# Decoder megakernel: earlier and smaller exchanges in cross-attention, four weight places in self-attention, and the bookkeeping of a top-k search moved to another engine

## The chip, the cores and the metric

The kernel runs on one core of one Trainium2 chip as a single launch. The metric is device time in microseconds. The engines are named as the profile names them: PE (matmuls; PEld is its weight load), DVE, ACT, POOL (GpSimd) and SP, which here only issues DMAs. ACT and POOL issue DMAs too. Each engine runs its own instructions strictly in order and waits on semaphores.

## The reference

Two decoder layers on x (4 batches of 512 tokens, 512 wide) with a layer norm behind each of six blocks. The change touches three of them:

```python
x = _layernorm(x + _L0_attn_ref(x, ...))                  # self-attention, 16 heads of 32   (touched)
x = _layernorm(x + _L0_xattn_ref(x, ctx_512, ctx_512))    # cross-attention                  (touched)
x = _layernorm(x + _L0_ffn_ref(x, ...))                   # ternary weights, 8-bit activations
x = _layernorm(x + _L1_attn_ref(x, ...))                  # self-attention                   (touched)
x = _layernorm(x + _L1_xattn_ref(ctx_512, x, ...))        # learned graph                    (touched)
x = _layernorm(x + _L1_ffn_ref(x, ...))                   # 16 experts, top 2

# cross-attention: queries are x itself, keys and values the context, no weights
H, KV = (32, 8); D = 16; G = H // KV
scores = einsum('bkgsd,bktd->bkgst', qh, kh) / sqrt(D); weights = softmax(scores, axis=-1)
out = einsum('bkgst,bktd->bkgsd', weights, vh)

# graph: keep the 153 largest of each row's 512, mix with x through gamma
topk_vals = lax.top_k(sim, 153)[0]; mask = sim >= topk_vals[:, :, -1:]
A = sigmoid(sim) * mask; A = (A + A.T) * 0.5
return (1 - gamma) * x + gamma * A
```

## The kernel before

The program is a row of stages, one behind another, each its own Python function with its own tiles and semaphores: self-attention (tiles `L_attn_...` in the profile, for both layers), cross-attention (`x_...`), FFN (`ffn_...`), self-attention again, graph (`graph_...`), experts. x itself stays in SBUF as the tile `X` (also called `XF`), 16 tiles of 128 tokens by 512.

**Self-attention** loads four 512x512 weight matrices one after another through two staging places `WS`, both inside the tile `PT` (L154). ACT rounds each to `WH` (L293), DVE subtracts to get the rest `WL` (L366), and SP may load the third and the fourth only when `WL` of the first and the second has been made. Order of the matrices: value, query, key, output. A list `plan`, written out by the host code, is the order in which PE, ACT and DVE go through their work.

**Cross-attention** works on 32 groups, g = 0 to 31: group g is batch g // 8 and key head j = g % 8, with four query heads. Operands are split in a high and a low part, since a product is made of three passes. Both parts of the transposed x of a batch (`XTH`, `XTL`, 1 MB each) are *exchanged*: SP writes them to DRAM (L707, L709), waits until they have landed (semaphore `x_out`), and reads them back, stacked by head, into `KS`-shaped rows: `stack_keys` (L726) for the context and `stack_queries` (L719) for x, the latter one group at a time, three groups ahead, into a ring `QS` of four places. In a group PE makes eight `max` units (L979: scores into `M`), DVE reduces each to the row's maximum (L919, `negm`), PE transposes the maxima (`mt`), DVE casts them to `mT` (L928), and SP sends `mT` as one more row of `QS` (`shift_row`, L732). Then PE makes the 16 score tiles `T` (L999), ACT takes their exponentials `PT` (L868), PE multiplies by V into `O` (L1008), ACT copies `O` to `OS` (L881), PE turns it (`turn`) and DVE divides into `Z`. L881 runs once for each group, so its rows are a clock of the groups.

The same `plan` puts the two units `xt` (PE's transposes of the next batch's x, L969, and DVE's and ACT's split of them) in group 4 of a batch. SP's exchange of it stands at the head of group 5. Ahead of group 0, SP loads the whole context (`CT`, `CTOK`, 1 MB each), exchanges its two parts and x of batch 0, and stacks keys, then queries.

Behind the last group of a batch, POOL adds x to `Z` (L828), and DVE makes the moments of the layer norm in small steps laid between its `max` reductions: four `bn_stats` (L94), then some twenty small operations (L64 to L77), two steps per `max` unit from the sixth unit on (`delay`, `pending`). POOL then applies the norm (L831). Between these, POOL sums the FFN weights and cuts twelve pieces of them to ternary (`cut_weights`, L815 to L822). ACT adds up absolute values of the same weights in 24 pieces (L874), four in each of groups 0 to 5.

**Graph**: a search by halving finds each row's threshold, for 16 tiles of rows at once, in 16 halvings (`HALVINGS`). In one halving DVE makes the middle of the interval (L1614), counts the elements above it in tiles 0 to 7 (L1617), ACT counts in tiles 8 to 15 (L1579), and DVE moves the ends (L1621, L1624, L1627, L1628):

```python
with dve.Fori(0, HALVINGS) as n:
    ve.tensor_tensor(mid[:], low[:], width[:], ALU.add).then_inc(q["mid_done"], 1)
    ...
    inst.then_inc(q["counted_v"], 1)
    dve.wait_ge(q["counted_v"], n + 1)
    ...
    dve.wait_ge(q["counted_a"], n + 1)
```

Behind it ACT takes sigmoids (L1595) and scales x (`XS`, L1599), DVE masks (L1650), PE transposes and DVE sums, mixes (L1665) and normalises.

## Time and profile before

| | us |
|---|---|
| median of 3 runs | 2621.11 (2618.74 to 2622.66) |
| the profiled execution, its own time | 2620.35 |
| its span | 2618.3 |
| L0 self-attention | 0 to 484.2 |
| cross-attention | 484.2 to 1044 |
| FFN | 1044 to 1439 |
| L1 self-attention | 1439 to 1920 |
| graph | 1920 to 2110 |
| experts | 2110 to 2618 |

The page gives PE 77% busy, PEld 52%, DVE 67%, ACT 48% and POOL 27% of the span. These are averages over stages with different limits: in cross-attention PE is busy 399.6 of 559.8 us and DVE 379.3, in the graph stage DVE 152.9 of 190, ACT 122.3 and POOL nearly nothing. A row of a timeline reads: start, duration (both us), engine, line, operation, what is written <- what is read, number of instructions, and in brackets the idle time ahead of it with what ended it.

### The profile page before, as it was taken

How to read it: one execution, taken by the hardware profiler on the slowest of the kernel's cores; microseconds unless marked ns; L12 is line 12 of the kernel's file. 1: busy time of each engine (PE TensorE's matmuls, PEld its weight loads, DVE VectorE, ACT ScalarE, POOL GpSimd, SP SyncE). 2: the span in 40 equal slices, each digit the busy share in tenths (PEclk: the TensorE clock that was granted, in tenths of full speed). 3: DMA queues.
4: the chain of work that ended last, by engine and by line, in shares of the span. 5: the costliest groups of instructions: out<-in, count | busy, mean ns of one | idle time of the engine just before them, and what ended most of it. 6: DMA issues, size and time to landing. Idle time of an engine off the chain costs nothing. (4 is left out here: it accounts for less than half of the span.)

```text
span 2618.3 us, 32959 instructions
## 1 busy us (share of the span) xinstructions
PE 2004.7 (77%) x12124; PEld 1350.8 (52%) x12156; DVE 1760.9 (67%) x2783; ACT 1258.8 (48%) x2244; POOL 718.3 (27%) x662
## 2 busy tenths in 40 slices
PE   5999999377778785888894699999910279879990
PEld 4778777222222221455552578777610157657770
DVE  3446565376768685799997445556568865379986
ACT  2323232177556564477777232323348541169881
POOL 1111222203595930211111120232200004055535
PEclk8899999688889888999996699999965589889995
DMA  5332321555352420400000432323110030099976
GB/s 153 83 72 53 70 60 39 159 149 152 85 157 73 147 51 10 175 1 1 1 1 1 121 71 52 73 50 74 25 64 0 0 116 1 1 387 422 415 285 192
DMA packets 84584, 264.55 MB, mean 101 GB/s; under 512 B 17504, under 2 KB 19040, under 8 KB 73424
## 3 DMA queue, kind: packets, MB, share of 16 engines
q0 software_dynamic: 29632, 151.50, 17.3%
q1 hardware_dynamic: 53776, 110.75, 14.9%
q8 instruction: 97, 1.59, 0.2%
q14 instruction: 55, 0.45, 0.1%
q10 hardware_dynamic: 1024, 0.26, 0.0%
HBM read 169.87 MB, written 41.72 MB: 81 GB/s over the span
## 5 line engine op out<-in xcount | busy, mean ns | idle before, releaser
L919 DVE TENSOR_REDUCE x_negm<-x_M 128x2 f32<-128x1024 f32 x256 | 309.3, 1223 | 111.3 <-PE x_M L979 110.8
L868 ACT ACTIVATE x_PT<-x_T 128x512 f32<-128x512 f32 x512 | 280.0, 598 | 197.3 <-PE x_T L999 192.0
L326 ACT ACTIVATE L_attn_PT<-L_attn_T 128x512 f32<-128x512 f32 x320 | 175.7, 595 | 359.5 <-PE L_attn_T L557 359.4
L407 DVE TENSOR_REDUCE L_attn_negm<-L_attn_M 128x2 f32<-128x1024 f32 (+1 forms) x192 | 192.2, 1040 | 58.6 <-PE L_attn_M L538 58.5
L233 POOL DMA_DIRECT2D L_attn_QKS<-L_attn_HL x64 | 34.9, 545 | 596.9 <-ACT L_attn_HL L311 563.1
L999 PE MATMUL x_T<-x_QS,x_KS 49*128 49x512 f32 x512 | 140.0, 544 | 64.7 <-ACT x_PT L868 44.9
L555 PE MATMUL L_attn_T<-L_attn_QKS 97*128 97x256 f32 (+3 forms) x512 | 166.8, 387 | 8.3 <-DMA L_attn_QKS<-L_attn_mT 6.2
L999 PEld LDWEIGHTS x_T<-x_QS,x_KS 49*128 49x128 f32 x512 | 51.8, 199 | 213.3 <-ACT x_PT L868 131.6
L536 PE MATMUL L_attn_M<-L_attn_QKS 96*128 96x384 f32 (+2 forms) x384 | 139.6, 434 | 28.8 <-DVE L_attn_XTL L381 11.5
L1008 PE MATMUL x_O<-x_PT,x_V 128*32 128x512 f32 x1024 | 153.4, 673 | 8.6 <-issue 8.4
L979 PE MATMUL x_M<-x_KS,x_QS 48*128 48x512 f32 x512 | 118.3, 459 | 42.6 <-DMA x_QS<-x_xl 22.8
L1567 PE MATMUL graph_P<-ident,graph_L 128*128 128x128 f32 x64 | 15.7, 427 | 172.6 <-DVE graph_L L1650 164.0
L2187 DVE TENSOR_TENSOR slots_WL<-slots_RAW,slots_WH 128x1024 fp32r<-128x1024 f32 x94 | 114.2, 1216 | 13.6 <-ACT slots_WH L2147 13.6
L557 PE MATMUL L_attn_T<-mask_kq,identr 128*128 128x128 f32 x512 | 121.8, 250 | 0.0
L2125 POOL DMA_INDIRECT slots_XG<-moe_x_rows,moe_slot_token x47 | 75.5, 1607 | 143.1 <-DVE slots_WL L2206 82.5
L555 PEld LDWEIGHTS L_attn_T<-L_attn_QKS 97*128 97x128 f32 x512 | 106.1, 207 | 15.3 <-DMA L_attn_QKS<-L_attn_mT 7.5
L435 DVE RECIPROCAL L_attn_AQ<-L_attn_DEN 128x512 f32<-128x512 f32 (+1 forms) x34 | 107.4, 3160 | 8.2 <-PE L_attn_O L581 8.2
L464 PE MATMUL L_attn_M<-L_attn_XTH,L_attn_WH 128*128 128x512 f32 x256 | 107.2, 419 | 6.1 <-DVE L_attn_WL L366 6.1
L557 PEld LDWEIGHTS L_attn_T<-mask_kq,identr 128*128 128x128 f32 x512 | 107.3, 210 | 0.2
L1579 ACT ACTIVATE graph_seen_a<-graph_SIM,graph_mid 128x512 bf16<-128x512 f32 x128 | 90.5, 708 | 32.5 <-DVE graph_mid L1614 18.9
L2147 ACT ACTIVATE slots_WH<-slots_RAW 128x1024 fp32r<-128x1024 f32 x94 | 94.2, 1058 | 22.6 <-DMA slots_RAW<-in_experts,moe_weight_row 22.6
L536 PEld LDWEIGHTS L_attn_M<-L_attn_QKS 96*128 96x128 f32 x384 | 81.3, 212 | 45.8 <-DVE L_attn_XTL L381 14.5
(389 smaller groups left out, 5528.3 us busy)
## 6 DMA issues: line engine op xcount, KB each, us to landing
L_attn_QKS<-L_attn_HL SPq DMA_DIRECT2D x192, 128.0 KB, 4.7
L_attn_QKS<-L_attn_HL POOLq DMA_DIRECT2D x192, 128.0 KB, 4.1
moe_y_rows<-slots_YS SPq DMA_DIRECT2D x47, 256.0 KB
x_WRAW<-in_w_gateT POOLq DMA_DIRECT2D x8, 1024.0 KB, 7.2
x_QS<-x_xh SPq DMA_DIRECT2D x128, 64.0 KB, 2.4
x_WRAW<-in_w_upT POOLq DMA_DIRECT2D x8, 1024.0 KB, 5.2
x_WRAW<-in_w_downT POOLq DMA_DIRECT2D x8, 1024.0 KB, 6.2
ffn_w<-x_WTER POOLq DMA_DIRECT2D x12, 512.0 KB, 3.5
```

The lines of the kernel that those rows point to most:

```text
L326: ac.activation(PT[:, s, bank], T[:, bank], ACT.Exp, scale=SCALE).then_inc(t_free, 1)
L407: last = ve.tensor_reduce(negm[:, g % 2, h0:h0 + nh, i], src, AX.X, ALU.max, negate=True)
L435: ve.reciprocal(AQ[:, cols], DEN[:, cols]).then_inc(inverted, 1)
L536: pe.matmul(m[:, c:c + w], QKS[0:R, r, 0, h, P * i:P * (i + 1)], QKS[0:R, r, 1, h, 0:w], start=True, stop=False)
L555: pe.matmul(T[:, c:c + w], QKS[0:R + 1, r, 1, h, P * j:P * (j + 1)], QKS[0:R + 1, r, 0, h, P * j:S], start=True, stop=False)
L557: last = pe.matmul(T[:, c:c + P], C["identr"][:], C["mask_kq"][:], start=False, stop=True)
L868: ac.activation(PT[:, s // 4, head(s), :], T[(STEPS_S * g + s) % 3][:], ACT.Exp, scale=SCALE).then_inc(t_free, 1)
L919: ve.tensor_reduce(negm[:, g % 2, u // 4:4:2, u % 4], m[:].rearrange("p (r k) -> p r k", r=2), AX.X, ALU.max, negate=True).then_inc(m_free, 1)
L979: last = pe.matmul(m[:, BANK * r:BANK * (r + 1)], QS[rows, g % 4, u // 4, P * (u % 4):P * (u % 4 + 1)], KS[rows, g % KV, :], start=True, s ...
L999: pe.matmul(T[(STEPS_S * g + s) % 3][:], KS[rows, g % KV, P * j:P * (j + 1)], QS[rows, g % 4, head(s) % 2, :], start=True, stop=True).then ...
L1008: last = pe.matmul(O[VW * h:VW * (h + 1), :], V[:, (g // KV) % 2, j, g % KV, :], PT[:, j, h, :], start=(j == 0), stop=(j == NT - 1))
L2187: ve.tensor_tensor(WL[t % 2][:, cols], RAW[t % RING][:, cols], WH[t % 2][:, cols].bitcast(F32), ALU.subtract).then_inc(up_lo, 1)
```

## The change

**Self-attention.** Four staging places instead of two: the second is the tile `V`, the fourth again the first. The key weights no longer wait for a `WL`; the output weights wait for the first; DVE writes `V` only when two `WL` are made.

**Cross-attention, head.** The context of batch 0 alone (256 KB) is loaded first; x of batch 0 is exchanged in halves, and only the first half is waited for; the context's keys of batch 0 are exchanged and stacked from ACT's queue; the rest of the context, of `CTOK` and of x follows behind the queries of group 2, and the exchange of the context's rest at g = 1, with DVE's split of it behind the first `turn` and ACT's at step 12 of group 0. PE waits for POOL's memsets only ahead of the first `max`. The 24 pieces of absolute sums move to groups 1 to 6.

**Cross-attention, exchange.** The `xt` units move to group 3 of a batch, the exchange into group 4 behind the queries of group g + 3, with no wait behind it; the wait for `x_out` and the keys come in group 5.

**Cross-attention, norm.** POOL's sum of x comes ahead of the ternary pieces, of which 2, 3 and 3 then stand ahead of the norm's application and 2, 1 and 1 behind it. The moments are one step per `max` unit and start at the fifteenth.

**Graph.** The loop is written out; each halving is two interleaved halves of 4 tiles for DVE and 4 for ACT; POOL does all the bookkeeping of the ends, and once a halving scales one tile of x in place, in place of ACT's 16 `XS`. Gamma is loaded and its sigmoid taken first.

```diff
-        if in_batch == 4 and s in (11, 13) and b + 1 < NB:
+        if in_batch == 3 and s in (11, 13) and b + 1 < NB:
...
-                sp.wait_ge(x_out, 32 * (b + 1))
...
+            unload_first_x(0)
+            sp.wait_ge(x_out, 32)
             stack_queries(0)
             stack_queries(1)
...
                 if j == 5 and b + 1 < NB:
-                    unload_x(b + 1)
-                    stack_keys(b + 1, 0, 4)
+                    sp.wait_ge(x_out, 32 * (b + 3))
+                    if b == 0:
+                        sp.wait_ge(ctx_out, 64)
+                    stack_keys(sp, b + 1, 0, 4)
                 if g + 3 < GROUPS:
                     stack_queries(g + 3)
+                if j == 4 and b + 1 < NB:
+                    unload_x(b + 1)
...
-            for b in range(NB - 1):
-                cut_weights((range(0, 2), range(2, 7), range(7, 12))[b])
+            for b, (ahead, behind) in enumerate(((range(0, 2), range(2, 4)), (range(4, 7), range(7, 8)),
+                                                 (range(8, 11), range(11, 12)))):
                 pool.wait_ge(m_free, drained("turn", KV * b + KV - 1))
                 gp.tensor_tensor(Z[b % 2][:], Z[b % 2][:], X[:, b, :, :], ALU.add).then_inc(added, 1)
+                cut_weights(ahead)
...
                     delay -= 1
                     if delay < 0:
-                        next(pending, None)
                         next(pending, None)
...
-                        delay, pending = 5, layernorm_moments(b)
+                        delay, pending = 14, layernorm_moments(b)
...
+        @block.gpsimd
+        def _(pool):
+            PER = 6
+            for g in range(2):
+                gp.tensor_tensor(side(mid, g), side(low, g), side(width, g), ALU.add).then_inc(q["mid_made"], 1)
+            for n in range(HALVINGS):
+                for g in range(2):
+                    step = Steps(pool, q["halving"], 2 * n + g, PER)
+                    pool.wait_ge(q["counted_v"], 2 * n + g + 1)
+                    step(gp.tensor_scalar(side(take, g)[:, 0], side(count, g)[:, 0], TOPK - 0.5, None, ALU.is_ge))
+                    pool.wait_ge(q["counted_a"], 2 * n + g + 1)
+                    step(gp.tensor_scalar(side(take, g)[:, 1], side(count, g)[:, 1], S + 1.5 - 2 * TOPK, None, ALU.is_le))
+                    step(gp.tensor_tensor(side(take, g), side(take, g), side(width, g), ALU.mult))
+                    step(gp.tensor_tensor(side(low, g), side(low, g), side(take, g), ALU.add))
+                    step(gp.tensor_scalar(side(width, g), side(width, g), 0.5, None, ALU.mult))
+                    step(gp.tensor_tensor(side(mid, g), side(low, g), side(width, g), ALU.add))
+                    pool.sem_inc(q["mid_made"], 1)
+                if n == 0:
+                    pool.wait_ge(q["gam2"], 2)
+                gp.tensor_scalar(XF[:, n, :], XF[:, n, :], g2[:, 0:1], 1.0, ALU.mult, ALU.mult).then_inc(q["scaled"], 1)
...
+            for n in range(HALVINGS):
+                for h in range(2):
+                    act.wait_ge(q["mid_made"], 2 * n + h + 1)
+                    for t in range(DVE_TILES + HALF * h, DVE_TILES + HALF * (h + 1)):
```

The order in which SP issues at the head of cross-attention; names are tiles and DRAM buffers, `x0_` is the prefix of the stage. Before:

```order
L701 DMA x0_CT<-in_ctxT 128x4x512
L702 DMA x0_CTOK<-in_ctx_512 128x16x128
L736 DMA x0_ch<-x0_CH 128x2048
L738 DMA x0_cl<-x0_CL 128x2048
L707 DMA x0_xh0<-x0_XTH 128x2048
L709 DMA x0_xl0<-x0_XTL 128x2048
L726 DMA x0_KS<-x0_ch 16x4x512
L726 DMA x0_KS<-x0_cl 16x4x512
```

After, the same queue:

```order
L712 DMA x0_CT<-in_ctxT 128x512
L723 DMA x0_xh0<-x0_XTH 128x1024
L725 DMA x0_xl0<-x0_XTL 128x1024
L734 DMA x0_QS<-x0_xh0 16x2x512 x2
L734 DMA x0_QS<-x0_xl0 16x2x512
```

The first queries stand behind 1.25 MB of other transfers instead of 6 MB and six DMAs of keys; the rest comes behind the queries of group 2.

SP's queue at the first exchange of a next batch. Before:

```order
L732 DMA x0_QS<-x0_mT 1x8x128 x2
L707 DMA x0_xh1<-x0_XTH 128x2048
L709 DMA x0_xl1<-x0_XTL 128x2048
L726 DMA x0_KS<-x0_ch 16x4x512
L726 DMA x0_KS<-x0_cl 16x4x512
L726 DMA x0_KS<-x0_ch 16x4x512 x2
```

After:

```order
L734 DMA x0_QS<-x0_xl0 16x2x512
L716 DMA x0_xh1<-x0_XTH 128x2048
L718 DMA x0_xl1<-x0_XTL 128x2048
L740 DMA x0_QS<-x0_mT 1x8x128 x2
L705 DMA x0_KS<-x0_ch 16x4x512
L705 DMA x0_KS<-x0_cl 16x4x512
```

A row of maxima (`mT`) now stands between the writing of x and the keys, and the wait for the written x stands behind that row.

POOL around the first norm of cross-attention. Before:

```order
L805 TENSOR_SCALAR x0_cut<-ffn_wmean 128x3 x2
L815 TENSOR_SCALAR x0_WTER<-x0_WRAW0,x0_cut 128x2048
L816 TENSOR_SCALAR x0_WTER<-x0_WRAW0,x0_cut 128x2048
L776 DMA x0_WRAW0<-in_w_gateT 128x2048
L820 TENSOR_TENSOR x0_WTER<-x0_WTER 128x2048
```

After:

```order
L822 TENSOR_SCALAR x0_cut<-ffn_wmean 128x3 x2
L845 TENSOR_TENSOR x0_Z0<-x0_Z0,X 128x2048
L832 TENSOR_SCALAR x0_WTER<-x0_WRAW0,x0_cut 128x2048
L833 TENSOR_SCALAR x0_WTER<-x0_WRAW0,x0_cut 128x2048
```

The sum of x (L845, L828 before) went from behind the first two ternary pieces to ahead of them.

## Rows read from the trace of the kernel before

**Rows 1.** Timeline of the head of L0 self-attention, ACT and DVE.

```profile
22.95 1.92 ACT L293 ACTIVATE L_attn_WH<-L_attn_PT 128x2048 fp32r<-128x2048 f32 x1 [5.51 <-DMA L_attn_PT<-in_L_attn_WkT]
...
25.39 0.69 DVE L389 TENSOR_TENSOR L_attn_V<-L_attn_M,L_attn_BR 128x512 f32<-128x512 f32 x1 [2.19 <-PE L_attn_M L464]
...
26.00 2.28 DVE L366 TENSOR_TENSOR L_attn_WL<-L_attn_PT,L_attn_WH 128x2048 fp32r<-128x2048 f32 x1
```

**Rows 2.** Timeline of the head of cross-attention, PE and SP.

```profile
493.50 3.68 PE L969 MATMUL x_M<-ident,X 128*128 128x128 f32 x16 [21.28 <-POOL x_V L770]
...
499.60 0.32 SPq L709 DMA_DIRECT2D x_xl<-x_XTL  x1
...
509.43 0.32 SPq L726 DMA_DIRECT2D x_KS<-x_ch  x1
...
519.97 1.22 PE L979 MATMUL x_M<-x_KS,x_QS 48*128 48x512 f32 x4 [22.79 <-DMA x_QS<-x_xl]
...
534.03 0.79 PE L999 MATMUL x_T<-x_QS,x_KS 49*128 49x512 f32 x2
```

**Rows 3.** Timeline of ACT's L881, once for each group: the clock of the groups.

```profile
613.60 0.62 ACT L881 ACTIVATE x_OS<-x_O 128x512 f32<-128x512 f32 x1
...
636.77 0.60 ACT L881 ACTIVATE x_OS<-x_O 128x512 f32<-128x512 f32 x1
...
677.45 0.61 ACT L881 ACTIVATE x_OS<-x_O 128x512 f32<-128x512 f32 x1
...
701.71 0.60 ACT L881 ACTIVATE x_OS<-x_O 128x512 f32<-128x512 f32 x1
...
745.95 0.60 ACT L881 ACTIVATE x_OS<-x_O 128x512 f32<-128x512 f32 x1
...
782.30 0.61 ACT L881 ACTIVATE x_OS<-x_O 128x512 f32<-128x512 f32 x1
...
809.02 0.60 ACT L881 ACTIVATE x_OS<-x_O 128x512 f32<-128x512 f32 x1
...
828.02 0.60 ACT L881 ACTIVATE x_OS<-x_O 128x512 f32<-128x512 f32 x1
```

**Rows 4.** Window of one undisturbed group: length, busy us of PE, PEld, DVE, ACT, POOL; clock.

```profile
714.82:727.94 13.12, 10.73 (x71) 3.63 (x69) 10.65 (x15) 9.07 (x19) 13.12 (x5) 1.00 0.11 31
```

**Rows 5.** Timeline of the first exchange, SP and PE.

```profile
615.10 0.32 SPq L726 DMA_DIRECT2D x_KS<-x_ch  x1
...
621.91 1.33 SPq L732 DMA_DIRECT2D x_QS<-x_mT  x2
...
630.48 0.79 PE L999 MATMUL x_T<-x_QS,x_KS 49*128 49x512 f32 x2 [5.53 <-DMA x_QS<-x_mT]
```

**Rows 6.** Timeline of DVE at the first norm of cross-attention.

```profile
681.11 1.42 DVE L94 BATCH_NORM_STATS2 x_x_ln_stats<-x_Z 128x6 f32<-128x512 f32 x2 [4.82 <-POOL x_Z L828]
```

**Rows 7.** Timeline of DVE in the search, one halving apart.

```profile
1947.27 0.17 DVE L1614 TENSOR_TENSOR graph_mid<-graph_low,graph_width 128x16 f32<-128x16 f32 x1 [0.37 <-DVE graph_width L1628]
...
1954.28 0.17 DVE L1614 TENSOR_TENSOR graph_mid<-graph_low,graph_width 128x16 f32<-128x16 f32 x1 [0.36 <-DVE graph_width L1628]
```

**Rows 8.** Groups by line and shape: line, engine, op, shapes xcount | busy us, mean ns | idle.

```profile
L1579 ACT ACTIVATE graph_seen_a<-graph_SIM,graph_mid 128x512 bf16<-128x512 f32 x128 | 90.5, 708 | 32.5 <-DVE graph_mid L1614 18.9 <-DMA graph_SIM<-graph_sim 13.6
...
L1617 DVE TENSOR_SCALAR_CACHE_REDUCE graph_seen_v<-graph_SIM,graph_mid 128x512 bf16<-128x512 f32 x128 | 86.6, 742 | 0.6
...
L1137 POOL TENSOR_SCALAR ffn_take<-ffn_count 128x8 f32<-128x8 f32 x18 | 4.3, 238 | 89.4 <-ACT ffn_CT L1177 88.5
...
L1146 POOL TENSOR_SCALAR ffn_XQF<-X,ffn_xscale 128x512 f32<-128x512 f32 x16 | 11.9, 741 | 15.6 <-DVE ffn_uscale L1261 12.8 <-POOL ffn_mid L1141 2.1 <-POOL ffn_mid L1130 0.4
...
L269 POOL TENSOR_SCALAR X<-X,L_attn_L_attn_ln_mean,L_attn_L_attn_ln_rstd 128x512 f32<-128x512 f32 x24 | 49.5, 2070 | 51.0 <-DVE L_attn_L_attn_ln_rstd L77 51.0
...
L1368 DVE TENSOR_SCALAR X<-X,ffn_mean,ffn_rstd 128x512 f32<-128x512 f32 x16 | 8.8, 548 | 0.6
```

**Rows 9.** Timeline of POOL's small operations beside DVE's L1368.

```profile
1430.33 0.53 POOL L1140 TENSOR_SCALAR graph_width<-graph_width 128x8 f32<-128x8 f32 x1
```

More of the change, by code:

```diff
@@ L159, in stage_self_attention @@
         DEN = ps("DEN", [P, BANK])
-        w_in = [sem("w_in0"), sem("w_in1")]
+        w_in = [sem(f"w_in{w}") for w in range(4)]
         w_hi, w_lo, b_in = sem("w_hi"), sem("w_lo"), sem("b_in")
@@ L247, in _ @@
             sp.dma_start(WS[1], wts[ORDER[1]]).then_inc(w_in[1], 16)
[L248 to L250 removed]
+            sp.dma_start(WS[2], wts[ORDER[2]]).then_inc(w_in[2], 16)
+            sp.wait_ge(w_lo, 1)
+            sp.dma_start(WS[3], wts[ORDER[3]]).then_inc(w_in[3], 16)
             sp.wait_ge(ones_set, 2)
@@ L695, in stage_cross_attention, with stack_keys @@
         drained = lambda kind, arg: at[kind, arg] + 3
+        def stack_keys(queue, b, lo, hi):
+            for r in range(2):
+                for n, part in enumerate((0, 1, 0)):
+                    rows = slice(LOW * r + HD * n, LOW * r + HD * (n + 1))
+                    src = CP[part][HD * lo:HD * hi, b, :].rearrange("(j d) s -> d j s", d=HD)
+                    queue.dma_start(KS[rows, lo:hi].bitcast(F32), src).then_inc(keys[lo], 16)
         block = ctx.enter_context(nc.Block())
@@ L719, in stack_queries @@
                         sp.dma_start(QS[rows, g % 4].bitcast(F32), src).then_inc(stacked[g % 4], 16)
-            def stack_keys(b, lo, hi):
-                for r in range(2):
-                    for n, part in enumerate((0, 1, 0)):
-                        rows = slice(LOW * r + HD * n, LOW * r + HD * (n + 1))
-                        src = CP[part][HD * lo:HD * hi, b, :].rearrange("(j d) s -> d j s", d=HD)
-                        sp.dma_start(KS[rows, lo:hi].bitcast(F32), src).then_inc(keys[lo], 16)
             def shift_row(g):
@@ L868, in _ @@
                     ac.activation(PT[:, s // 4, head(s), :], T[(STEPS_S * g + s) % 3][:], ACT.Exp, scale=SCALE).then_inc(t_free, 1)
-                    if g < 6 and s % 4 == 2:
-                        piece = 4 * g + s // 4
+                    if 1 <= g < 7 and s % 4 == 2:
+                        piece = 4 * (g - 1) + s // 4
                         c, half = piece // 2, piece % 2
@@ L956, in _ @@
         def _(t):
-            t.wait_ge(ones_set, 4)
             for x in plan:
@@ L1544, in stage_graph @@
         PP = [ps(f"P{i}", 2 * BANK) for i in range(4)]
-        names = ("loaded mid_done counted_v counted_a gam gam2 "
-                 "sigm xs masked turned summed halved z_done stat norm shifted applied between")
+        names = ("loaded mid_made counted_v counted_a halving scaled gam gam2 "
+                 "sigm masked turned summed z_done stat norm shifted applied between")
         sim_in = [sem(f"sim_in{b}") for b in range(NB)]
@@ L1595, in _ @@
                     ac.activation(SIGM[:, i, :], SIM[:, b * NT + i, :], ACT.Sigmoid).then_inc(q["sigm"], 1)
-                if b:
-                    act.wait_ge(q["z_done"], b * NT)
-                for i in range(NT):
-                    ac.activation(XS[:, i, :], XF[:, b * NT + i, :], ACT.Identity, scale=g2[:, 0:1]).then_inc(q["xs"], 1)
             act.wait_ge(q["shifted"], 1)
@@ L1630, in _ @@
-            dve.wait_ge(q["gam"], 1)
-            pre = Steps(dve, q["gam2"], 0, 2)
-            pre(ve.tensor_scalar(g2[:], gamma[:], -1.0, 2.0, ALU.mult, ALU.add))
-            pre(ve.tensor_scalar(gh[:], gamma[:], 0.5, None, ALU.mult))
+            for n in range(HALVINGS):
+                for h in range(2):
+                    dve.wait_ge(q["mid_made"], 2 * n + h + 1)
+                    for t in range(HALF * h, HALF * (h + 1)):
+                        inst = ve.tensor_scalar(seen_v[:, t, :], SIM[:, t, :], mid[:, t:t + 1], 0.0, ALU.is_ge, ALU.add,
+                                                accum_out=count[:, t:t + 1])
+                    inst.then_inc(q["counted_v"], 1)
+                if n == 0:
+                    dve.wait_ge(q["gam"], 1)
+                    pre = Steps(dve, q["gam2"], 0, 2)
+                    pre(ve.tensor_scalar(g2[:], gamma[:], -1.0, 2.0, ALU.mult, ALU.add))
+                    pre(ve.tensor_scalar(gh[:], gamma[:], 0.5, None, ALU.mult))
```

132 lines of the change are left out of this document (70 added, 62 removed).

## The prediction

> **What bounds the kernel now.** I read the page's busy shares first, then the windows of the stages, then, stage by stage, the waits and timelines at the places that the diff touches. No engine is full over the whole span, and stages follow each other strictly, so a time saved ahead of a stage's last instruction is saved for the program. In L0 self-attention the head is what matters: ACT rounds the key weights at 22.95, DVE adds the values' bias at 25.39 and makes `WL` at 26.00, with no idle time between the two on DVE [rows 1]. In cross-attention the clock is ACT's copy of each group's output, L881 [rows 3]. An undisturbed group takes 13.12 us, of which DVE works 10.65 [rows 4]. Everything beyond 13.12 in an interval is a stall, which makes this the view that sizes the terms below. The stage ahead of the groups shows PE idle for 21.28 and again for 22.79 us [rows 2]. The graph stage repeats with a period of 1954.28 − 1947.27 = 7.01 us [rows 7], in which ACT counts for 8 × 0.708 = 5.66 and DVE for 8 × (0.742 less the overlap of neighbours) [rows 8]. So ACT's counting bounds a halving, and 1.35 us of bookkeeping lie bare between two.
>
> The sum is made against the profiled execution, 2620.35 us. The median of the runs is 2621.11, 0.03% above it.
>
> **Weight places: 0.** The key weights would land before 22.95 in the new version (ACT sat idle 5.51 us for them [rows 1]), so their rounding comes earlier. But the plan is unchanged: DVE's `WL` of the keys stands behind the bias addition of 25.39 and starts when that ends. ACT's rounding ended at 24.87, already before 25.39. So the DMA wait is not the last one and nothing moves. Bounds: a gain of at most the 26.00 − 22.95 = 3 us by which this `WL` trails the arrival of the weights, in each of two stages, if DVE's order is not what holds it, against +1 us for DVE's new wait ahead of the first `V`. I take 0.
>
> **Head of cross-attention: −12.5 (−5 to −20).** Before, PE's transposes start at 493.50, held by POOL's memset. SP has x's second part under way at 499.60, all has landed at 509.43, keys and queries are issued, and the first `max` runs at 519.97, the first score at 534.03, 14.06 later [rows 2]. The wait for the memset moves to the first `max`, so the transposes start with the stage, about 484.5. Half of x leaves after half of them and the splits, about 3.5 us on, and takes about half of 509.43 − 499.60 = 9.8, so 5. The queries took 519.97 − 509.43 = 10.5 with six key DMAs ahead of them on the same queue, and about 8 without. That gives 484.5 + 3.5 + 5 + 8 = 501 for the first `max`, 19 earlier, and 515 for the first score. The keys come from ACT's queue meanwhile. Not all of that stays. 4.5 MB (rest of context, tokens and x, raw weights) now run beside groups 0 to 2, ahead of `shift_row(1)` on SP. DVE's split of three batches of context stands in group 1, and ACT's rounding in group 0. I put 7 back: 1.7 and 1.4 for the two pieces of work that moved in, by their sizes, and 4 for a queue held behind the bulk, which is less than half of what 2 MB of x took above. −19.4 + 7 = −12.5. The ends are no give-back and one twice as large.
>
> **Exchange: −27 (−18 to −30).** In the first exchange the interval is 636.77 − 613.60 = 23.17, 10.05 too much. In the second the two intervals are 782.30 − 745.95 = 36.35, 36.35 − 2 × 13.12 = 10.11 too much [rows 3]. The third is like the second. What ends last is SP: the keys' DMAs go out at 615.10, after the wait for x to have landed, the row of maxima only at 621.91, and PE's first score has waited 5.53 for that row at 630.48 [rows 5]. After the change nothing on SP waits for x between its writing and the row of its own group; the wait is one group, 13 us, later, and x took under 10 us to land. All of 10.05 + 2 × 10.11 = 30.3 is reachable. Left over: in group 5 the keys' six DMAs still stand ahead of the queries, and in group 4 the wait for the `xt` split is cheap only if the split is done, which group 3 now gives. I leave 1.1 for each, so −27. The cost of the `xt` units themselves (the interval before each exchange) moves to group 3 with them and is no gain. Lower end: 4 us left in each exchange, the part of the DMAs of 616 to 622 that has not gone.
>
> **POOL's order and the moments: −14 (−7 to −19).** Intervals with a norm are 701.71 − 677.45 = 24.26 and 828.02 − 809.02 = 19.00, so 11.14 and 5.88 too much, with the third like the second: 22.9 [rows 3]. In the first, DVE waited 4.82 for POOL's sum of x, which stood behind two ternary pieces [rows 6]. With the sum first that wait goes, save what POOL's weight sums leave; they end well before. The rest is DVE work (four `bn_stats` of 0.7 and some twenty of 0.17, 6.5 in all) laid into a group and a half. One step per unit and a later start spread it over three groups. DVE has 13.12 − 10.65 = 2.5 us to spare in each, but not where each unit needs it, so I leave half: 3 × 2.9 = 8.7. 22.9 − 8.7 = 14.2. Behind the norm POOL applies, which nobody in the groups waits for. POOL's last pieces lie beside the last batch's eight groups; that cover is over 100 us long for four pieces, and if it were gone each would cost what it takes.
>
> **Graph: −20.5 (−22 to −8).** If ACT counts without a pause, 15 boundaries give (7.01 − 5.66) each, 20.3, and start and end cancel to within 0.5. This needs POOL to be quick enough. While ACT counts one half (2.83) POOL has to do the other half's six operations, and once in a halving the scaling as well. The same kind of chain stands in the FFN stage at 0.238 a piece [rows 8]: six of them with their hand-over come to 1.85. The scaling is like L1146, 0.741; the slowest of its size is L269 at 2.07 [rows 8]. Even so 1.85 + 2.07 + 1.85 = 5.77 is the ACT time within 0.1. Taking 16 `XS` off ACT behind the search gives nothing by itself, since ACT waited for DVE there.
>
> In the trace, though, a small POOL operation takes 0.53 instead of 0.24 beside DVE's L1368 [rows 9]. At this pace a half takes 2.9 to 3.1 and a halving 2 × 3.05 + 2.07 + hand-overs = 8.8: the whole gain and 28 us of loss. Which of the two DVE operations the counting resembles decides. L1368 does its 128x512 in 0.548, the count in 0.742 [rows 8], so it is another, slower mode, and most of the FFN's chains ran beside a busy DVE at 0.24. I take the fast case. The Trainium skill, page "SBUF — State Buffer", section "SBUF: two separate sides", says that DVE and GpSimd share a port pair as an exclusive lock, which DVE takes only in a two-port mode or with two inputs from SBUF, and that the loser is blocked for the whole instruction. By that rule the counting, with one input and at the slow rate, would not hold POOL, and the trace's one stretched row beside the fast L1368 agrees.
>
> **Sum.** 0 − 12.5 − 27 − 14.2 − 20.5 = −74.2, so 2620.35 − 74.2 = 2546.
>
> **Rivals.**
> - *The head gives nearly nothing and the exchange keeps a third.* The bulk behind the queries holds SP's queue, the saved 19 are given back, and each exchange keeps 4 to 6 us because the row of maxima now queues behind 2 MB of x. For it: rows of maxima have been the last wait already [rows 5]. 2546 + 12 + 10 = 2568, in a band of 2560 to 2575. Chance 0.15.
> - *POOL bounds the search at the pace of rows 9.* 16 × (8.8 − 5.66) = 50 more than in the sum: 2596. Against: the mode of the count. Chance 0.07.
> - *Slower: POOL gets in only between DVE's counts.* If the counting does hold the pair, each of POOL's 12 small operations waits for the end of a count, 12 × 0.742, then the scaling 2.07: with hand-overs about 11.5 us a halving, 16 × (11.5 − 5.66) = 93 above the sum: 2639. It makes the whole slower from 5.66 + 74/16 = 10.3 us a halving. The rule named above, turned round, would be this case, and the trace shows no count beside POOL, so it can't be excluded. Chance 0.03.
> - *The weight places do give*, 3 us in each of two stages: 2540. For it: PE waits for that `WL`. Against: DVE's row at 25.39. Chance 0.08, inside the main band.
> - *The head keeps all 19 and the norm all but a trifle*: 2546 − 7 − 6 = 2533. Chance 0.1.
>
> **How the numbers follow.** The forecast with its own spread, 2536 to 2560, has 0.57; with the weights' case 0.65. The head rival has 0.15, the good one 0.1, POOL's two 0.1. To hold 8 in 10 the range goes from 2532 to 2573: it takes in the head rival and most of the good one and leaves POOL's out. About 0.2% is what a measurement of this kernel can tell from no change, 5 us. Only POOL's slowest case and mishaps in two places at once come near it: faster 0.96, same 0.01, slower 0.03.
>
> **What would show it.** L881's intervals: 13.1 in groups 4 to 6 of a batch but for the one with `xt`, and 16 instead of 24 and 19 at a norm. PE's first `max` at 501 and first score at 515. In the graph, ACT's counting rows 5.66 us apart per halving with no idle time on POOL's `mid`, and POOL's small operations at 0.25. The key `WL` at 26.0 as before. Wrong would be: POOL's rows in the search at 0.5 or more, ACT idle for them, SP's `mT` row late in group 4 or in groups 1 and 2.

## The result, and the profile after

The changed kernel takes 2607.11 us in the median of 8 runs (2600.37 to 2611.98), against 2621.32 of the kernel before on the same chips (8 runs, 2615.18 to 2628.51). The ratio is 0.9935 with a 95% interval of 0.9917 to 0.9954: 17 us faster, 12 to 22, where 74 were forecast. The profiled execution took 2610.24 us, its span is 2608.5.

By stage, the two traces say: L0 self-attention ends at 488.1 (484.2 before), cross-attention takes 565.7 us (560.0 before), and the graph search, from the first count to the first mask, takes 92.0 instead of 113.7. Search and weight places by themselves are worth what was forecast (cross_undone below), so the missing 57 us belong to cross-attention, which did not become shorter at all.

**The weights** [answers to rows 1]. Timeline of the changed kernel, ACT and DVE:

```profile
18.29 1.91 ACT L294 ACTIVATE L_attn_WH<-L_attn_PT 128x2048 fp32r<-128x2048 f32 x1 [0.76 <-DMA L_attn_PT<-in_L_attn_WkT]
...
26.32 2.28 DVE L367 TENSOR_TENSOR L_attn_WL<-L_attn_PT,L_attn_WH 128x2048 fp32r<-128x2048 f32 x1
```

The key weights are rounded 4.7 us earlier, and their `WL` starts at 26.32 instead of 26.00: the DMA wait was not the last one, as forecast.

**The head** [answers to rows 2]. Timeline of the changed kernel; L1005, L1017 and L1037 are what L969, L979 and L999 were:

```profile
488.19 3.67 PE L1005 MATMUL x_M<-ident,X 128*128 128x128 f32 x16 [12.14 <-DVEq L916]
...
498.11 0.79 SPq L734 DMA_DIRECT2D x_QS<-x_xh  x2
...
510.14 1.22 PE L1017 MATMUL x_M<-x_KS,x_QS 48*128 48x512 f32 x4 [18.29 <-DMA x_QS<-x_xl]
...
524.15 0.80 PE L1037 MATMUL x_T<-x_QS,x_KS 49*128 49x512 f32 x2
...
539.67 1.48 ACT L893 ACTIVATE x_CH<-x_CT 128x1536 fp32r<-128x1536 f32 x1 [4.45 <-DMA x_CT<-in_ctxT]
...
541.69 0.79 PE L1037 MATMUL x_T<-x_QS,x_KS 49*128 49x512 f32 x2 [3.50 <-ACT x_PT L899]
```

Reckoned from the stage's start (488.1 and 484.2), the first `max` comes 13.7 us earlier, not 19, and so does the first score. Then ACT waits 4.45 us for the rest of the context inside group 0, and PE 3.50 behind it.

**The groups** [answers to rows 3 and 4]. Windows of the changed kernel from one L912 (L881 before) to the next: bounds, length, busy us (and instructions) of PE, PEld, DVE, ACT and POOL, granted clock of PE, DMA share, GB/s:

```profile
550.99:571.85 20.86, 17.65 (x71) 5.38 (x71) 12.45 (x16) 13.22 (x27) 1.07 (x2) 0.58 0.56 178
...
706.52:729.94 23.42, 18.45 (x87) 7.45 (x87) 16.30 (x28) 10.90 (x20) 1.57 (x2) 0.71 0.28 102
...
743.04:756.14 13.10, 10.71 (x71) 3.62 (x69) 10.85 (x20) 9.58 (x19) 5.00 (x3) 1.00 0.42 70
...
827.53:862.96 35.43, 23.04 (x87) 9.00 (x87) 28.87 (x28) 10.90 (x20) 19.44 (x7) 0.55 0.41 155
...
862.96:882.62 19.66, 18.61 (x71) 5.65 (x71) 11.42 (x23) 9.08 (x18) 0.00 (x0) 0.51 0.40 58
```

The exchange intervals behind `xt` are 13.10 in the second batch (36.35 for two before), as the step wanted. But the `xt` intervals of the second and third batch are 23.42 and 35.43 where they were 18.0, and the third norm has one of 22.41 (968.59 to 991.00; the expectation of quiet_pool below takes it for an `xt` interval, which it is not). The last line shows a whole group at 19.66 with a granted clock of 0.51, almost exactly half: PE waits at most 0.3 us at a time in it, and it is 6.5 us longer.

**The norm** [answers to rows 6]. Timelines of DVE and POOL of the changed kernel in the interval of 35.43:

```profile
825.67 4.46 DVE L66 TENSOR_TENSOR x_x_ln_var<-x_x_ln_stats 128x4 f32<-128x4 f32 x1
...
831.18 5.30 DVE L67 TENSOR_SCALAR x_x_ln_mean<-x_x_ln_mean 128x4 f32<-128x4 f32 x1
...
836.52 3.64 DVE L68 TENSOR_TENSOR x_x_ln_tmp<-x_x_ln_tmp 128x4 f32<-128x4 f32 x1
...
843.62 3.49 DVE L70 SCALAR_TENSOR_TENSOR x_x_ln_var<-x_x_ln_tmp,x_x_ln_var 128x4 f32<-128x4 f32 x1
```

```profile
826.02 4.08 POOL L837 TENSOR_TENSOR x_WTER<-x_WTER 128x2048 bf16<-128x2048 bf16 x1
...
831.00 5.45 POOL L832 TENSOR_SCALAR x_WTER<-x_WRAW,x_cut 128x2048 bf16<-128x2048 f32 x1
836.43 5.43 POOL L833 TENSOR_SCALAR x_WTER<-x_WRAW,x_cut 128x2048 bf16<-128x2048 f32 x1
...
843.01 4.07 POOL L837 TENSOR_TENSOR x_WTER<-x_WTER 128x2048 bf16<-128x2048 bf16 x1
```

Four operations on four columns, 0.17 us each before, take 4.46, 5.30, 3.64 and 3.49. Three of them end within 0.05 us of the POOL operation beside them: 830.13 and 830.10, 836.48 and 836.45, 847.11 and 847.08. The fourth, L68 with two inputs, ends at 840.16, 1.70 us ahead of the end of POOL's L833. DVE was held by POOL's ternary pieces. Over the stage the 120 moment operations take 64.4 us instead of 29.7, ten of them over 0.8.

**The search** [answers to rows 7 and 8]. Groups and tile rows of the changed kernel; the tile rows give minimum, median and maximum in ns, and the first and last start:

```profile
L1641 ACT ACTIVATE graph_seen_a<-graph_SIM,graph_mid 128x512 bf16<-128x512 f32 x128 | 90.2, 711 | 10.6 <-DMA graph_SIM<-graph_sim 10.6
L1612 POOL TENSOR_TENSOR graph_mid<-graph_low,graph_width x32: 199/200/202, 1949.1 to 2036.5; 128x8 f32<-128x8 f32 x32
L1616 POOL TENSOR_SCALAR X<-X,graph_g x16: 690/695/1186, 1952.3 to 2036.9; 128x512 f32<-128x512 f32 x16
```

ACT counts 128 tiles in 90.2 us with no idle time but for the first load. POOL's operations beside the counts stay at 0.20 and the scaling at 0.695; the one scaling of 1.186 runs at 2036.87, beside DVE's mask (L1697, 2036.74) and not beside a count. The step did what was forecast.

### The profile page after: what moved, and what is told of

It is laid out like the page before. It is cut to its first block and busy times, and to the rows that moved or that the text cites. A ratio compares the mean times of both kernels' runs of the same rounds, so it can differ in the third digit from the quotient of the medians.

```text
span 2608.5 us, 32953 instructions
## 1 busy us (share of the span) xinstructions
PE 2028.3 (78%) x12124; PEld 1358.0 (52%) x12156; DVE 1776.8 (68%) x2704; ACT 1247.2 (48%) x2229; POOL 771.2 (30%) x872
## 5 line engine op out<-in xcount | busy, mean ns | idle before, releaser
L1037 PE MATMUL x_T<-x_QS,x_KS 49*128 49x512 f32 x512 | 144.2, 560 | 50.1 <-ACT x_PT L899 46.1
L1046 PE MATMUL x_O<-x_PT,x_V 128*32 128x512 f32 x1024 | 162.8, 712 | 6.8 <-issue 6.6
L1017 PE MATMUL x_M<-x_KS,x_QS 48*128 48x512 f32 x512 | 124.0, 482 | 48.4 <-DVE x_negm L954 29.8
L1037 PEld LDWEIGHTS x_T<-x_QS,x_KS 49*128 49x128 f32 x512 | 53.3, 205 | 202.6 <-ACT x_PT L899 136.3
L466 PE MATMUL L_attn_M<-L_attn_XTH,L_attn_WL 128*128 128x512 f32 x256 | 104.8, 409 | 0.0
```

The source lines that it names most:

```text
L466: inst = pe.matmul(out, lhs(a, k), rhs(a, k), start=(k == 0 and a == 0), stop=(k == KC - 1 and a == 2))
L1017: last = pe.matmul(m[:, BANK * r:BANK * (r + 1)], QS[rows, g % 4, u // 4, P * (u % 4):P * (u % 4 + 1)], KS[rows, g % KV, :], start=True, s ...
L1037: pe.matmul(T[(STEPS_S * g + s) % 3][:], KS[rows, g % KV, P * j:P * (j + 1)], QS[rows, g % 4, head(s) % 2, :], start=True, stop=True).then ...
L1046: last = pe.matmul(O[VW * h:VW * (h + 1), :], V[:, (g // KV) % 2, j, g % KV, :], PT[:, j, h, :], start=(j == 0), stop=(j == NT - 1))
```

## The experiments

All ratios are against the kernel before, run in turn with the kernel on the same chip.

| kernel | ratio, 95% interval | in us of 2621 |
|---|---|---|
| changed | 0.9935 (0.9917 to 0.9954) | −17 |
| norm_alone | 1.0049 (1.0025 to 1.0074) | +13 |
| exchange_alone | 1.0015 (0.9997 to 1.0033) | +4 |
| cross_undone | 0.9924 (0.9896 to 0.9951) | −20 |
| graph_undone | 0.9976 (0.9954 to 0.9998) | −6 |
| norm_undone | 0.9971 (0.9946 to 0.9995) | −8 |
| pace_undone | 1.0069 (1.0043 to 1.0094) | +18 |
| quiet_pool | 0.9849 (0.9799 to 0.9898) | −40 |
| quiet_late | 0.9880 (0.9849 to 0.9911) | −31 |
| quiet_453 | 0.9875 (0.9836 to 0.9915) | −33 |
| quiet_no_exchange | 0.9867 (0.9830 to 0.9903) | −35 |
| quiet_no_head | 0.9845 (0.9816 to 0.9875) | −41 |
| quiet_old_weights | 0.9833 (0.9780 to 0.9886) | −44 |
| light | 0.9791 (0.9769 to 0.9813) | −55 |
| light_no_exchange | 0.9885 (0.9861 to 0.9908) | −30 |
| loads_on_sp | 0.9806 (0.9783 to 0.9828) | −51 |

The interval of quiet_pool alone is 13 us to either side. A difference between it and another kernel of the table is therefore known only to some 14 to 19 us either way (the half widths of the two, added in squares), and smaller ones are not shown by the ratios.

### Is it POOL beside the moments, or the pace of the moments?

**quiet_pool** puts every ternary piece behind the norm's application and the moments back to the old pace:

```diff
-            for b, (ahead, behind) in enumerate(((range(0, 2), range(2, 4)), (range(4, 7), range(7, 8)),
-                                                 (range(8, 11), range(11, 12)))):
+            for b, behind in enumerate((range(0, 4), range(4, 8), range(8, 12))):
...
-                cut_weights(ahead)
...
+                        next(pending, None)
-                        delay, pending = 14, layernorm_moments(b)
+                        delay, pending = 5, layernorm_moments(b)
```

> The changed kernel with two edits: the moments go back to two steps per unit from the sixth unit on, and all ternary pieces (four per batch) stand behind the application of the norm; the sum of x stays ahead. Theory PORT: POOL's long operations on ternary pieces (5.45 us each) lay beside DVE's small moment operations and held them up to 5.3 us each. Without that overlap no small operation is over 0.8 us, their total in the groups is about 30 us instead of 64.4, a norm costs 6 us in its group, the xt group 18 instead of 23, 35 and 22, and the program is 35 to 42 us faster than the changed kernel: about 2568. Rival PACE: the loss comes from one step per unit running into the group with the xt units; it expects the same here, and differs in the next run.

Measured: 2568.28 us, 1.51% under the kernel before. The 120 moment operations take 29.6 us, none over 0.8. The `xt` intervals are 17.96 and 18.01 in the second and third batch.

**pace_undone** has the last three lines of that diff alone, the pace of the moments.

> The changed kernel with the moments alone put back to two steps per unit from the sixth unit on; POOL still works on ternary pieces between its sum of x and the application of the norm. Theory PORT: the moments now fall fully beside POOL's pieces, small operations of 3 to 5 us stay or grow in number, and the program is within 10 us of the changed kernel, 2600 to 2615, or slower. Rival PACE: the collision with the xt units is gone, xt groups take 18 us, and the program is at 2570.

Measured: 2627.78 us, 1.0069. So PACE falls: the old pace with POOL's pieces beside it is worse than the change. Timeline of DVE in it:

```profile
830.63 3.64 DVE L70 SCALAR_TENSOR_TENSOR x_x_ln_var<-x_x_ln_tmp,x_x_ln_var 128x4 f32<-128x4 f32 x1
...
847.06 5.70 DVE L76 TENSOR_SCALAR x_x_ln_tmp<-x_x_ln_tmp 128x4 f32<-128x4 f32 x1
```

Its 120 moment operations take 107 us, 97.9 of them in the first three norms, and 24 are over 0.8. It and quiet_pool differ only in where POOL's pieces stand, and so in whether POOL works or waits while DVE makes the moments, and lie 2.2% apart, 58 us.

**norm_alone** makes the same point from the other side, the kernel before with this part of the diff and nothing else.

> The kernel before with the norm part alone: sum of x ahead, two, three and three pieces between sum and application, one moment step per unit from the fifteenth on. PORT: stretched small operations as in the changed kernel in each of three norms, a dozen of 3 to 5 us, against a gain of 5 to 10 for the sum ahead: 10 to 25 us slower than before, 2631 to 2646. If the spread of the moments is what I forecast, 14 us faster: 2607.

Measured: +13 us (7 to 19), nine operations over 0.8 us and 59.9 us of moments in all. The part that was to bring 14.2 costs 13 by itself, in the kernel before.

**norm_undone** is the changed kernel with the norm part as before.

> The changed kernel with the norm part undone: pieces 0 and 1, 2 to 6 and 7 to 11 stand ahead of the sums of x as before, and the moments are at the old pace. PORT: no stretched small operation, since POOL waits between sum and application; but the absolute sums come a group later in this kernel, so the first sum stands behind two pieces until about 703 and DVE waits for it some 15 us in the first norm. So slower than quiet_pool by 10 to 15: about 2580. If the sum behind the pieces costs nothing, it equals quiet_pool.

Measured: 8 us under the kernel before, so 32 above quiet_pool (18 to 46), not 10 to 15, and 9 above the changed kernel (1 to 17). The wait that had been expected is there and larger. Waits of PE in it (waiting line, releaser, us in all, times, longest):

```profile
PE x_M L1028 <- DVE x_negm L954: 30.4, 2, 21.2
```

The first sum of x stands behind two pieces which themselves come a group later, since the absolute sums moved to groups 1 to 6. So the parts hang together: with the absolute sums moved, the sum of x had to go ahead, and in that company the norm part, which costs 13 by itself, is worth these 9.

### The search and the weights

**graph_undone** and **cross_undone** take one stage function of the kernel before each.

> The changed kernel with the graph stage of the kernel before. The search in the changed trace runs at 5.7 us a halving without idle time on ACT, so undoing it costs what I forecast for it: 20 us more than the changed kernel, which puts this kernel 0 to 5 us above the kernel before. If the cross-attention accounts for the whole 14 to 17 us of the result and the search for nothing, it stays where the changed kernel is.

> The changed kernel with the cross-attention stage of the kernel before, so the search and the weight places alone: 20 us faster than before if both of these steps are as forecast (search 20, weight places 0). With up to 4 us of loss in the self-attention stages, as the changed trace might be read (its first stage ended 3.8 us later), 12 to 16.

Measured: cross_undone 20 us under the kernel before, so search and weights together are worth what was forecast. graph_undone is 11 us above the changed kernel by the two ratios (3 to 18) instead of 20, just outside. The traces of the search itself leave no doubt on its size: from ACT's first count to the first mask it takes 92.0 us in those of the changed kernel, cross_undone and quiet_pool and 113.6 and 113.7 in those of graph_undone and the kernel before. Its cross-attention, whose code is the same as in the changed kernel, ran 18 us faster in its trace (550.58 to 1018.78 from first to last L912, against 550.99 to 1037.70). Such a spread between executions of the same code is the size of several terms, so a single trace sizes nothing of cross-attention below 20 us.

**quiet_old_weights** is quiet_pool with the self-attention of before.

> quiet_pool with the two weight places of before in both self-attention stages. Forecast of this step 0: the key weights' WL starts at about 26 us in both. Same time as quiet_pool within its interval; the rival, 3 us in each stage, would make it 6 slower, and a loss as in the end of the first stage (3.8 later) would make it 4 to 8 faster.

Measured: 0.9833 against 0.9849, within the intervals, which at 19 us either way can't tell 0 from the rival's 6. The traces can: the last operation on x of L0 self-attention ends between 483.2 and 486.8 in the four with the old places and between 482.1 and 487.6 in the thirteen with the new. The 3.8 us by which the first stage ended later in the changed trace lie within this spread.

### The exchange

**exchange_alone** moves it in the kernel before:

```diff
-                if in_batch == 4 and s in (11, 13) and b + 1 < NB:
+                if in_batch == 3 and s in (11, 13) and b + 1 < NB:
...
                 if j == 5 and b + 1 < NB:
-                    unload_x(b + 1)
+                    sp.wait_ge(x_out, 32 * (b + 2))
                     stack_keys(b + 1, 0, 4)
                 if g + 3 < GROUPS:
                     stack_queries(g + 3)
+                if j == 4 and b + 1 < NB:
+                    unload_x(b + 1)
```

> The kernel before with the exchange alone moved: xt units in group 3, x written out in group 4 behind the queries, waited for in group 5. Forecast of this step: 27 us, at most 30; the two intervals behind each xt interval at 13.1 to 14 us instead of 23.2, and 21.4 with 14.9. Where a norm's moments do not reach the xt group, as here, nothing is given back.

Measured: 1.0015, nothing gained. Yet PE's waits for the row of maxima fell, over the groups, from the first of these lines (kernel before) to the second (exchange_alone). The third and fourth are from the timeline of exchange_alone:

```profile
PE x_T L999 <- DMA x_QS<-x_mT: 19.7, 5, 6.3
```

```profile
PE x_T L1001 <- DMA x_QS<-x_mT: 7.4, 4, 2.5
...
685.85 1.12 PE L991 MATMUL x_M<-ident,x_OS 128*128 128x128 f32 x4 [9.86 <-DVE x_negm L921]
...
787.78 0.80 PE L1001 MATMUL x_T<-x_QS,x_KS 49*128 49x512 f32 x2 [2.26 <-DMA x_QS<-x_mT]
```

Where it went: at the norm of the first batch PE waits 9.86 instead of 4.50 for DVE, which waits for POOL's sum of x. DVE could start on it at 683.25, against 681.11 before, although the groups were ahead: a group that comes earlier only waits longer. And a wait of 2.26 us for a row in a quiet stretch is followed by an interval of 17.38 and one of 14.42, 5.6 us too much for the two. Windows of exchange_alone, first these two, then one later where nothing is waited for over a microsecond:

```profile
776.70:794.08 17.38, 13.11 (x71) 4.30 (x69) 10.50 (x15) 9.07 (x19) 16.72 (x6) 0.80 0.57 151
794.08:808.50 14.42, 12.32 (x71) 4.09 (x71) 10.14 (x14) 9.07 (x18) 13.79 (x5) 0.89 0.50 149
...
829.44:849.10 19.66, 18.61 (x71) 5.67 (x71) 12.07 (x26) 9.08 (x18) 6.63 (x4) 0.50 0.07 20
```

Every interval of 13.1 with all 71 matmul rows has a granted clock of 1.00; where it is 0.50, the same work takes 19.66. A stall costs its length and, in this loop, then what the lower clock costs afterwards.

**quiet_no_exchange** undoes the exchange in quiet_pool.

> quiet_pool with the exchange undone: xt units in group 4, x written at the head of group 5 with the wait behind it. By the forecast of this step 27 us slower than quiet_pool. By exchange_alone, which gained nothing, 0 to 8 slower. My reading of exchange_alone: the waits for the row of maxima fell from 19.7 to 7.4 us, but a norm's wait for POOL's sum grew by 5 and three groups ran at the lower clock by the history of stalls; so with a quiet norm the step is worth 12 to 20.

Measured: 0.9867 against 0.9849, 5 us with 16 either way, where 12 to 20 had been expected. The forecast 27 is out of reach, the expected 12 is not excluded. That something still eats a part also with a quiet norm is told by rows of SP, POOL and PE of quiet_pool in group 23:

```profile
886.51 1.33 SPq L740 DMA_DIRECT2D x_QS<-x_mT  x2
```

```profile
886.10 0.81 POOL L792 DMA_DIRECT2D x_WRAW<-in_w_downT  x1 [0.30 <-POOL x_WTER L833]
```

```profile
892.56 0.50 PE L1036 MATMUL x_T<-x_QS,x_KS 49*128 49x512 f32 x2 [1.87 <-DMA x_QS<-x_mT]
```

POOL sends for the next 1 MB of weights 0.4 us ahead of SP's row of maxima, and the row, 8 KB, releases PE only 6.0 us later; the median landing of the DMAs into this tile is 2.4. The same pair stands at 869.11 and 869.20 (wait 1.94) and at 756.52 and 755.95 (1.22). In all traces together a row and a 1 MB load of POOL's queue were sent within 0.6 us of each other 14 times. PE waited for the row every time, 0.2 to 2.4 us, and got it 4.4 to 6.5 us behind SP's row; the wait of 2.26 in exchange_alone above is one of them (row 781.35, load 781.50). In the kernel before, the same loads run beside the groups too; a row that is late inside the exchange's long wait costs nothing more.

**light** leaves these loads out but for a sliver, so the ternary weights, and all that follows from them, are not the reference's; **light_no_exchange** also undoes the exchange.

```diff
+                if c >= 12:
+                    dst, src = (dst[:, :, 0:16], src[:, :, 0:16]) if c % 12 >= 8 else (dst[:, 0:64], src[:, 0:64])
```

> quiet_pool with POOL's second loads of the FFN weights (ten of 1 MB, beside the groups) cut to 64 of 2048 columns; the ternary weights and so the result are not the reference's. Theory LOAD: a row of maxima that SP sends within a microsecond of such a 1 MB load lands 5 to 6 us later instead of 2.4, PE waits 2 to 3 us for it, and the group and the next one run partly at the lower clock (17 and 14.5 us instead of 13.1). Without the loads PE's waits for the row of maxima behind group 8 are under 1 us in all (8.7 in quiet_pool with the first groups) and the program is 5 to 12 us faster than quiet_pool. If the lower clock comes by itself, intervals of 14.5 to 17 stay.

> light with the exchange undone as in quiet_no_exchange (result not the reference's, for the same reason). If LOAD is what ate the exchange's gain, undoing the exchange costs here what I had forecast, 20 to 30 us, since nothing else collides. If the exchange is worth little in itself, the two are within 8 us.

Measured: 0.9791 and 0.9885, 0.94% or 25 us apart (16 to 33), with intervals that are clear of each other. With nothing in the row's way the exchange brings what it was forecast to bring (27). From group 8 on, light shows no wait for the row. quiet_pool and light differ by 0.58%, 15 us (1 to 29), though the waits for the row that went are 8.7 us at most; that the rest is the lower clock behind them fits the windows above, and was not measured apart.

**loads_on_sp** keeps the work whole and takes the ten loads to SP, each behind a row:

```diff
+                load = {12: 2, 13: 3, 15: 4, 16: 5, 20: 6, 21: 7, 23: 8, 24: 9, 29: 10, 30: 11}.get(g)
+                if load is not None:
+                    sp.wait_ge(compared, 2 * (load - 1))
...
+                    sp.dma_start(dst, FW["chunks"][load]).then_inc(raw_again[load % 2], 16)
```

> quiet_pool with the same ten 1 MB loads issued by SP, each right behind a row of maxima, in groups 12, 13, 15, 16, 20, 21, 23, 24, 29 and 30, so that none is ahead of a row. LOAD expects the waits for the row of maxima behind group 8 gone as in light, and 4 to 12 us less than quiet_pool. Rival: the queries of the next group queue behind 1 MB on SP's queue and PE waits for them instead.

Measured: 2556.56 us, 0.9806 (0.9783 to 0.9828), 51 us under the kernel before and the lowest ratio of the kernels that compute the whole. From quiet_pool's it is 11 us away with 14 either way, so that this edit makes the kernel faster is likely and not shown; that it takes the waits away is. The waits for the row behind group 8 come to 0.2 us (5.9 in quiet_pool), and no queries are waited for. Its windows of two norms, the same work both times:

```profile
673.96:688.61 14.65, 11.00 (x71) 3.70 (x69) 14.04 (x32) 9.07 (x18) 0.00 (x0) 1.00 0.09 27
...
908.19:927.62 19.43, 16.54 (x71) 4.96 (x69) 14.14 (x32) 9.08 (x19) 0.00 (x0) 0.65 0.08 21
```

DVE's work is 14.0 and 14.1, no wait of PE is over 1.0 us in either, and PE is busy 5.5 us longer at the lower clock: the 4.8 us between them go with the clock. What lowered it in the second, no run here shows.

### The head

**quiet_late** puts the rest of the context off by two groups and cuts 4, 5 and 3 pieces; **quiet_453** has only the pieces; **quiet_no_head** is quiet_pool with the head of before.

```diff
-                    if g == 0 and s == 12:
+                    if g == 2 and s == 12:
...
-                    if arg == 0:
+                    if arg == 2:
```

> quiet_pool with the rest of the context put off: ACT's rounding of it from group 0 to group 2, DVE's split from the turn of group 0 to that of group 2, its exchange from group 1 to group 3, and ternary pieces 4, 5, 3 behind the three norms. Theory: ACT's wait of 4.45 us for the context in group 0 and the split in group 1 made PE run at the lower clock through groups 0 and 1 (intervals 26.8 from first score and 20.9); without them group 0 takes 20 and group 1 13.8, and 3 us come back in groups 2 and 3: 10 to 12 us faster than quiet_pool, some 52 us under the kernel before. Rival: the bulk transfers themselves slow the first groups, then the intervals stay at 20 and only 2 us are won.

> quiet_pool with the ternary pieces 4, 5, 3 instead of 4, 4, 4 behind the three norms, the context as in the changed kernel. In quiet_pool POOL's last pieces ran beside the last groups and DVE's last sum took 4.33 us instead of 2.29; here they end 17 us earlier. Expected 2 to 4 us faster than quiet_pool, about 1.6% under the kernel before. If quiet_late was slower than quiet_pool because of its 4, 5, 3 and not because of the context's later exchange, this kernel is 8 us slower than quiet_pool.

> quiet_pool with the head of cross-attention as before (whole context first, x in one piece, keys from SP, absolute sums in groups 0 to 5, PE waiting for the memsets). Forecast of this step: 12.5 us slower than quiet_pool, between 5 and 20. By the traces the first score comes 13.7 us earlier after the stage's start in the changed kernel and 15 are given back in groups 0 to 2, so if these traces are typical there is no difference, 0 to 3.

Measured: quiet_no_head 0.9845 against 0.9849, no difference, with 15 us either way. The ratios alone would still allow the forecast 12.5; the traces don't. Counted from the last operation on x of L0 self-attention, the first L912 (ACT's copy of a group's output, whatever its line in the kernel at hand) comes after 62.2 to 64.0 us in the twelve traces with the new head and after 70.7 to 74.7 in the five with the old. The first interval behind it is 18.2 to 21.0 in all twelve and 13.8 in all five, and the third L912 comes after 95.0 to 104.4 in the former and 98.3 to 102.3 in the latter. The lead is gone two groups on. Windows of quiet_no_head and of quiet_pool, the interval behind the first L912 (559.62 in the former, 549.37 in the latter):

```profile
559.62:573.44 13.82, 10.76 (x71) 3.64 (x69) 10.74 (x15) 12.97 (x26) 1.07 (x2) 1.00 0.50 167
```

```profile
549.37:570.36 20.99, 18.02 (x71) 5.56 (x71) 12.44 (x16) 13.22 (x27) 1.07 (x2) 0.58 0.56 176
```

quiet_pool is 10 us ahead at the first and 3 ahead at the sixth (636.86 and 640.21; 87.5 us for five intervals against 80.6). quiet_late did not repair it, as its rival in the expectation had it: without ACT's wait for the context, group 0 to 1 still took 19.66 at a clock of 0.52, and PE waited 4.89 us in group 4 for a row that SP had sent at 614.48, behind x (2 MB from 605.4 on) and 2.2 us behind a 1 MB load of POOL. By ratio quiet_late, quiet_453 and quiet_pool can't be told apart. Which cause keeps the clock low in the first two groups of the new head stays open: the bulk transfers, the waits of 1.8 us or the shorter time at work before.

## Why the prediction was wrong, point by point

- **Weight places, 0.** Right, with its reason (DVE's order, not the load, is last): `WL` at 26.32, and no shift of the stage's end over 17 traces.
- **Head, −12.5 (−5 to −20).** Wrong, 0 by traces and by ratio. The first score came 13.7 us earlier, not 19: the transposes began with the stage, as forecast, but SP's first queries stood 10.0 us behind its start, not 8.5, and took 12.0 us from there to the first `max` (498.11 to 510.14) where I had 8. The larger miss is the give-back, and the step that failed is "I put 7 back". It prices work moved in and a held queue, and not the clock. Group 0 gave back 7.0 (26.8 us from first score to first L912, against 19.8) and the interval behind it 7.1 more, at a granted clock of 0.58. The term also has a slip: 519.97 − 501 is 19.0 and not 19.4, so the sum should have had −12.
- **Exchange, −27 (−18 to −30).** The mechanism and the size were right (25 us with the loads out of the way), but not in a kernel with them: a loss of 4 (−1 to 9) in the kernel before, a gain of 5 with 16 either way in quiet_pool. The step that failed is "I leave 1.1 for each": I took the row of maxima to be free once SP's queue was, and did not ask what POOL's queue sends at the same moment. In the kernel before, the wait for POOL's sum of x, which grew by 5.4 us, took its share too.
- **POOL's order and the moments, −14 (−7 to −19).** Wrong in sign: +13 alone, and quiet_pool shows 23 us (9 to 36) between the changed kernel and the same without the overlap, at the old pace. Beside the moved absolute sums the part is worth 9 (norm_undone), because without it the sum of x comes too late. The step that failed is "behind the norm POOL applies, which nobody in the groups waits for". I counted what DVE waits for, not what POOL does in the time in which it had waited before: 30 us of idle POOL had become two or three pieces of 15 us of work, right beside the small operations of DVE.
- **Graph, −20.5.** Right: 20 with the weights by ratio (cross_undone, 13 to 27), 21.7 by trace, though only 11 (3 to 18) by the ratio of graph_undone. The counts did not hold POOL, and the rivals of a slow POOL fell.
- **The sum.** 0 + 0 + 0 to −5 + 13 − 20 gives −7 to −12; measured −17 (−12 to −22), which the intervals of the parts cover. The parts are not independent, as norm_undone shows, so that this sum comes near is in part luck. All three errors lie in one stage and have one form: a wait was taken away, and what else runs in that time was not priced.

The rule that would have told the third of them stood in the prediction, at the wrong place. The Trainium skill, page "SBUF — State Buffer", section "SBUF: two separate sides", has the port pair of DVE and GpSimd as an exclusive lock that is held for a whole instruction. I weighed it where DVE would hold up POOL, in the search, and not where POOL's long operations would hold up DVE. The rows above agree that DVE is held: a 0.17 us operation ends 0.03 us behind a POOL operation of 5.45. They do not agree on the whole instruction: L68, with two inputs, was let go 1.70 us before L833 ended, and here the measurement decides.

## What to carry to other kernels

When work is moved into time in which an engine had waited, ask what the other engine did in that time because the first one was quiet: small operations of DVE beside long ones of POOL cost up to the length of the long ones (5.70 us for one of 0.17 here). Before taking away a long wait in a steady loop, list every transfer and wait that it covered, on all queues; what lands by chance in the open is then waited for at each place. And price a stall of TensorE by the interval and the one behind it, with their granted clock, not by the idle time in brackets: here the two intervals at a wait of 2.3 us were 5.6 too long.

## What was not expected of the hardware

- An operation of DVE on 128x4 took up to 5.70 us beside POOL's 128x2048 operations; single-input ones (L67, L76) as well as those with two inputs. When it is let go follows a pattern, in all 43 operations over 0.8 us of the changed kernel, pace_undone and norm_alone. The 17 with one input, and the 13 with two beside POOL's bf16 `tensor_tensor` (4.1 us), end 0.01 to 0.04 us behind the POOL operation. The 13 with two inputs beside POOL's fp32 to bf16 `tensor_scalar` (5.45 us) end 1.69 to 1.71 us before it does. `bn_stats` on 512 columns stayed at 0.67 to 0.71 there. POOL beside DVE's counts (0.742 us each, 128 of them) was not slowed.
- An 8 KB transfer sent by SP within 0.6 us of a 1 MB transfer of POOL's queue released its reader 4.4 to 6.5 us later in 14 cases of 14, against a median landing of 2.4.
- The granted clock decides as much as the waits: the same group takes 13.1 us at 1.00 and 19.66 at 0.50, and stayed low for two groups of exchange_alone (808.50 to 849.10, 0.56 and 0.50) with no wait of PE over 1.1 us. Two executions of the same cross-attention code differed by 18 us between the first and the last group.
